# Row maxima from the high parts alone, as two 64-row matmuls issued together

## What is computed

```
xt = transpose(x)                        # 1024 tokens x 512
qh = (xt @ Wq.T) split into 8 heads of 64
scores = qh @ qh.T / 8                   # per head, 1024 x 1024
logits = (scores * cmask + (1 - cmask) * -1e30) * rmask
ctx = softmax(logits) @ qh
out = x + transpose(ctx @ Wo.T)
```

## Time and profile before

| what | value |
|---|---|
| median of three runs | 1601.06 us |
| span of the profiled execution | 1599.3 us |
| TensorE matmul busy | 1513.2 us, 95% |
| TensorE weight load busy | 1185.6 us, 74% |
| GpSimd busy | 1336.3 us, 84% |
| VectorE busy | 1198.6 us, 75% |
| ScalarE busy | 877.7 us, 55% |

### The profile page before, as it was taken

One profiled execution on the slowest core, in us unless ns is written; L12 is line 12 of the kernel. 1 busy time (PEld: TensorE's weight loads), 2 busy tenths in 40 slices (PEclk: granted clock), 3 DMA queues, 4 the chain that ended last, 5 costly groups with the idle time before them and its releaser, 6 DMA issues. The chain is left out here.

```text
span 1599.3 us, 32587 instructions
## 1 busy us (share of the span) xinstructions
PE 1513.2 (95%) x10636; PEld 1185.6 (74%) x10636; DVE 1198.6 (75%) x2676; ACT 877.7 (55%) x2189; POOL 1336.3 (84%) x1078
## 2 busy tenths in 40 slices
PE   5789999999999999999999999999999999999985
PEld 4568777777777777777777777777777777777753
DVE  4487787878778787877878787787878778787753
ACT  4345556565655656565565656556565655656441
POOL 3377989898898989889898988989898898988875
PEclk9779999999999999999999999999999999999998
DMA  4423444544444454444445444444554444454411
GB/s 137 104 65 96 108 120 109 130 123 111 118 113 117 112 130 123 110 118 115 116 113 130 123 110 119 114 117 111 130 123 111 119 113 117 111 130 96 111 53 55
DMA packets 93809, 179.07 MB, mean 112 GB/s; under 512 B 24704, under 2 KB 24832, under 8 KB 93632
## 3 DMA queue, kind: packets, MB, share of 16 engines
q1 hardware_dynamic: 64448, 109.71, 29.2%
q0 software_dynamic: 29184, 67.17, 14.9%
HBM read 36.77 MB, written 33.55 MB: 44 GB/s over the span
## 5 line engine op out<-in xcount | busy, mean ns | idle before, releaser
L835 ACT ACTIVATE small_Pt<-scores,small_kbias 108x270 f32<-108x270 f32 x1280 | 550.9, 483 | 343.7 <-PE scores L1245 334.8
L985 DVE TENSOR_REDUCE small_mxp<-max_scores 108x1 f32<-108x270 f32 x1280 | 546.7, 435 | 250.7 <-PE max_scores L1226 228.9
L646 POOL TENSOR_TENSOR small_Pacc<-small_Pacc,small_Pt 108x540 f32<-108x540 f32 x384 | 520.8, 1356 | 122.3 <-ACT small_Pt L835 116.6
L1226 PE MATMUL max_scores<-small_ops 128*108 128x270 f32 x1280 | 420.1, 336 | 22.2 <-DVE small_mxp L985 21.6
L1257 PE MATMUL ctx_psum<-small_Pt,small_V 108*64 108x270 f32 x2560 | 317.5, 395 | 0.0
L1017 DVE RECIPROCAL small_rsum<-small_rsum 128x67 f32<-128x67 f32 (+1 forms) x512 | 240.8, 532 | 66.3 <-ACT small_rsum L771 66.3
L1242 PE MATMUL scores<-small_ops 128*108 128x270 f32 x1280 | 281.1, 294 | 8.7 <-ACT small_Pt L835 7.0
L1226 PEld LDWEIGHTS max_scores<-small_ops 128*108 128x108 f32 x1280 | 221.3, 175 | 89.9 <-issue 38.4
L1257 PEld LDWEIGHTS ctx_psum<-small_Pt,small_V 108*64 108x64 f32 x2560 | 187.4, 139 | 109.0 <-issue 4.6
L1245 PE MATMUL scores<-small_ops 128*108 128x270 f32 x1280 | 265.4, 289 | 0.0
L1242 PEld LDWEIGHTS scores<-small_ops 128*108 128x108 f32 x1280 | 193.5, 174 | 38.4 <-ACT small_Pt L835 20.1
(11 more groups left out here) (129 smaller groups left out, 2273.2 us busy)
## 6 DMA issues: line engine op xcount, KB each, us to landing
small_ops<-small_H SPq DMA_DIRECT2D x512, 135.0 KB, 2.5
small_ops<-small_L SPq DMA_DIRECT2D x256, 135.0 KB, 2.5
small_ops<-small_mrow SPq DMA_DIRECT2D x128, 2.1 KB
small_xg<-x_rows,small_idx POOLq DMA_INDIRECT x80, 3.9
small_xtail<-x_rows,small_idx POOLq DMA_INDIRECT x80, 5.0
out_rows<-small_xtail,small_idx POOLq DMA_INDIRECT x80, 3.7
out_rows<-small_xg,small_idx POOLq DMA_INDIRECT x80, 4.1
wqT_sb<-wqT SPq DMA_DIRECT2D x1, 1024.0 KB, 5.4
```

The source lines that it names most:

```text
L646: nc.gpsimd.tensor_tensor(acc, other, t["Pt"][:R, p0], ALU.add).then_inc(pacc_step, 1)
L835: nc.scalar.activation(t["Pt"][:R, (NT * s + k) % f.NP, half, :], ST[(2 * (NT * h + k) + half) % 3][:R, 0:H], ACT.Exp, bias=t["kbias"][:R, ...
L985: nc.vector.tensor_reduce(t["mxp"][:R, h % 2, m // 2, m % 2:m % 2 + 1], MX[m % 2][:R, 0:H], AX.X, ALU.max).then_inc(mx_red, 1)
L1226: nc.tensor.matmul(MX[m % 2][:R, 0:H], ops[:, OPA, tile_cols(m // 2)], ops[:, OPB, half_cols(m % 2)], start=True, stop=True).then_inc(mx_r ...
```

## The change

`max_scores` now takes both operands from OPB, the high parts, and so leaves the low part out of the shifts (the scores themselves keep it). The halves of the queries are two matmuls of 64 array rows: half 0 on partitions 0 to 63 and half 1 on 64 to 127, each into its own bank. The two are issued together, behind one wait for both banks: `mx_red` must count 2k reductions of this head, where half 0 before waited for 2k - 1 and half 1 for 2k. In `batch` the pair stands behind the scores of the step and ahead of the jobs' first part. The two heads ahead of the loop are changed in the same way. VectorE's reductions and everything else stay as they are.

```diff
-                def max_scores(s, s4, h, m):
-                    ops = t["ops"][:, h % SLOTS]
-                    if m == 0:
+                def max_scores(s, s4, h, k):
+                    ops = t["ops"][:, h % SLOTS, OPB]
+                    if k == 0:
                         pe.wait_ge(put_max_ops[h % SLOTS], 64 * (s4 + 1))
-                    at_least(pe, mx_red, 2 * NT * s + m - 1)
-                    nc.tensor.matmul(MX[m % 2][:R, 0:H], ops[:, OPA, tile_cols(m // 2)], ops[:, OPB, half_cols(m % 2)],
-                                     start=True, stop=True).then_inc(mx_ready, 1)
+                    at_least(pe, mx_red, 2 * NT * s + 2 * k)
+                    for half in range(2):
+                        rows = slice(DK * half, DK * half + DK)
+                        nc.tensor.matmul(MX[half][:R, 0:H], ops[rows, tile_cols(k)], ops[rows, half_cols(half)],
+                                         start=True, stop=True).then_inc(mx_ready, 1)
...
-                        for m in range(2 * NT):
-                            max_scores(0, 0, 0, m)
+                        for k in range(NT):
+                            max_scores(0, 0, 0, k)
...
                 for m in range(2 * NT):
-                    max_scores(1, 0, 1, m)
+                    if m % 2 == 0:
+                        max_scores(1, 0, 1, m // 2)
...
                             ahead = h < HEADS - 2 or has_next
+                            scores(s, (HEADS // 2) * b + h // 2, h, k)
                             if ahead:
-                                max_scores(s + 2, 2 * b + (h + 2) // SLOTS, h + 2, 2 * k)
-                            scores(s, (HEADS // 2) * b + h // 2, h, k)
+                                max_scores(s + 2, 2 * b + (h + 2) // SLOTS, h + 2, k)
                             misc(table[h, k], b, par, s, 0)
-                            if ahead:
-                                max_scores(s + 2, 2 * b + (h + 2) // SLOTS, h + 2, 2 * k + 1)
```

## The result

The changed kernel takes 1768.19 us in the median (1767.31 to 1769.26), beside 1602.24 us for the kernel before on the same chip: a ratio of 1.1042, with a 95% interval of 1.1022 to 1.1061. It is slower, as forecast, and inside the range of 1595 to 1798. But it is 51 us above the forecast of 1717 and outside that case's own range of 1684 to 1735. The profiled span grew from 1599.3 to 1767.5 us.

The account below looks back on a forecast made before the run. TensorE's instruction stream was taken to bound the kernel. Changes of shape less the pair's saving, 504 steps (+111 us) and 126 steps (+5), made +116 on 1599.3: 1715, or 1717 us as a median; range 1595 to 1798.

Parts of the forecast that it names:

- that case's own range: Range of the main forecast alone, 1684 to 1735 us around 1717; that case had a chance of 0.58.
- What bounds the kernel: TensorE's instruction stream sets the end: 98% busy in fourteen sequences, so changed distances between matmul starts enter the time directly.
- TensorE for nobody: Other engines wait for TensorE, which hardly waits: its matmuls waited 10.0, 9.2 and 4.0 us in 1306 us.
- The saving of the pair: At max_scores, two 64-row halves run side by side for one matmul's cost: 0.12 us for each of 630 pairs, 76 us.
- The two changes of shape in a step: Around the max_scores pair, 0.16 us going in and 0.18 back; less the pair's saving, +116 us in all.
- hides the stricter wait: Steps 0.2 us longer give VectorE slack, hiding the pair's wait for both reductions; without that cover, 20 us more.
- rival 2: The pair's halves don't overlap in loads or products, so the saving is gone: +191 us, 1793 us; chance 0.10.
- Rival 1: Row groups don't change the array's shape as columns do, so only the saving stays: 1525 us, up to 1545; chance 0.20.
- Rival 3: Array need not be emptied, but weights of another shape load uncovered, 0.09 us a change: +26, 1627 us; chance 0.12.
- What would show it: Timeline signs: late pair load, pair starts within 0.01 us, plain step 0.22 us longer, TensorE's wait for VectorE not growing.

Follow-up runs that it names:

- the 64-row twin ahead of the scores: Changed kernel with its 64-row pairs moved ahead of the scores and VectorE doing both reductions of a step before its jobs: 1722.7 us.
- the full twin: Changed kernel with full 128-row matmuls, both halves together ahead of the scores, and VectorE doing both reductions before a step's jobs: 1604.4 us.
- the first experiment: Changed kernel with full 128-row matmuls (OPA against OPB), both halves still together behind the scores and one wait: 1701.8 us, ratio 1.062.

## Why the prediction was right, and where it was off

- **What bounds the kernel**: right in the main. TensorE is at 92% of a longer span, and the others wait for it (VectorE 473.9 us before its reductions instead of 228.9). But "TensorE for nobody" holds no longer: its matmuls of max_scores waited 47.3 us in the fourteen sequences.
- **The saving of the pair**: right in kind. The two row groups run side by side, 0.003 us apart. Taking that away cost 57 us where I had 76, because a part of the longer step fell into waits.
- **The two changes of shape in a step**: the mechanism is shown for row groups. The loads start 0.215 behind the matmul before, not with it; the split into 0.09 for emptying and 0.09 for an uncovered load is the same as for columns; issued twice, the pair's second turn costs 0.13. My net sum of 116 us stands against the measured 121, a hit in size: the mean of a change came out at 0.154 to 0.171 us, and I had 0.16 and 0.18. From one start of the scores to the next, the 64-row twin ahead of the scores is 0.22 us longer in the median of the 40 steps of a sequence, as I had for a plain step; 28 of the 40 grow by 0.2 or more, and 5 by less than 0.1 or not at all. The dense stretch alone has 0.255. By that price the sum would be 135, or 160 for the twins ahead of the scores, and both are more than was measured. A part of the reason is in the timeline of the full twin:

```profile
622.40 0.48 PE L1229 MATMUL max_scores<-small_ops 128*108 128x270 f32 x2
622.71 0.41 PE L1245 MATMUL scores<-small_ops 128*108 128x270 f32 x2
```

  Here the two full matmuls take 0.31 us to the scores, not 0.25, and over the 560 steps the second starts 0.181 behind the first in the mean, not 0.125. So full matmuls have delays of their own at this place, and a change of shape that falls on one does not add its whole price. My sum left these overlaps out. That it was so near with prices below those of the dense stretch is partly luck: one omission against the other.
- **The step that failed** is the sentence that a longer step "hides the stricter wait", with its bound of 20 us if the cover is missing. The new order's wait cost 45 us (46 by the other way). The cover is there, but it is half of what was needed: with full matmuls the same order costs 100 us, with steps 0.2 us longer 45. I had looked at VectorE's mean load (0.87 us of reductions in a step of 2.3) and at the one wait that existed. What counts is what stands in VectorE's queue between a step's two reductions, 2.2 us of jobs in the view above (565.54 to 567.71), and that each reduction starts later because its product now comes behind four scores matmuls. I also took it that scores ahead of max_scores costs nothing; moving half 0 alone costs 30 us in the kernel before.
- **The range**: 1768 lies above this case's own range, whose upper end was 1735, and inside the whole range only because that reached up to rival 2's price. That it holds the result is luck, since neither rival 2 nor a wait of 45 us was what I forecast.
- **Rival 1** (faster, 1525) fell: the loads start 0.215 us late. **Rival 2** (the halves don't overlap) has a price near the result, 1793, but nothing of it happened: the two start 0.003 us apart. **Rival 3** (no emptying) fell too: 0.09 us of the 0.215 is emptying. The tiling page of the Trainium skill (TensorEngine Tiling (Array Packing), Tiling Modes) says that a change of mode drains the engine; the traces agree for rows as for columns, 0.09 us each time.
- **What would show it**: the load 0.2 us behind the scores, the 0.3 us from the pair to the next full matmul and the pair's two starts within 0.01 us came as written. The pair's own start did not: I had 0.28 us behind the last scores matmul, and its row starts with its load, 0.215 behind, so that the load lies inside the row (0.37 us long instead of 0.285). A sequence grew by 10.2 us (143/14) instead of 7. "TensorE's wait for VectorE doesn't grow" was wrong, and one of my own signs of a wrong prediction came true: the idle time before max_scores rose by 57 us, "tens of us".

## What to carry over

Tiles of the array pay only if enough work stays in one shape: here a change of shape and back took 0.38 us in a dense stretch and 0.31 to 0.34 in the mean, and one paired matmul saves 0.12. By these numbers some three pairs in a row would be needed to break even; that is an estimate, no kernel here tried it. Before moving an instruction in a hand-written order, write down what the consumer's in-order queue holds between the two events that the producer will now wait for together; its mean load does not show that. And count waits from starts to starts, since a pipelined matmul's row hides the first 0.16 us of each.

## What the hardware showed unexpectedly

Two of VectorE's instructions, each of which reads two tensors in SBUF, did not have a fixed duration. L1085 (108 partitions, 512 elements), the same instruction with the same operands in each kernel, took 886 ns in the mean before, 1017 ns in the changed kernel, 1236 ns in the first experiment and 757 ns in the full twin ahead of the scores; L1022 took 1.90 us at 565.89 above, and 850 ns in the mean before. L1081, which reads a bank of PSUM, stayed at 741 to 742 ns in all four, and L1017, a reciprocal with one operand in SBUF, at 531 to 533.

The traces show what ran beside the long ones: tensor operations on GpSimd, and for L1022 it matters who started first. In the changed kernel 33 of the 64 executions of L1022 began while such an operation was running; they took 1307 ns in the mean. Seventeen had one begin beside them later and took 709 to 712, and 14 had none and took 709 to 711. In the kernel before it is 897 ns in the mean for 48, and 708 to 712 for the 15 beside which GpSimd began later. In both kernels the time above 0.71 us follows what was left of GpSimd's operation almost exactly (correlation above 0.99). L1085 in the changed kernel took 1414 ns in the 30 executions that met one and 752 in the other 45. No run moved GpSimd's work alone, so this is read from traces, not tested by a change.

It bears on the waits: in the changed kernel's fourteen sequences 182 pairs start more than 0.01 us late behind the scores, 59.6 us in all. Fourteen of them, one in the sixth head of each sequence, wait behind a stretched L1022, which accounts for at most 15.6 us (an estimate: its time above 0.71 us).
